# Second attention layer: row-tiled products in six runs per batch, the other products between them in a new order

## The chip, the cores and the metric

The kernel runs on one core of a Trainium2 chip. Its time is the device time of one execution in microseconds (us); the kernel before takes 1221.17 us, the median of three runs between 1220.6 and 1221.69. The core has five engines with a queue each: TensorE (PE; its weight loads are shown apart as PEld), VectorE (DVE), ScalarE (ACT), GpSimd (POOL) and SyncE (SP), which here only starts transfers. Each runs its own instructions in order and waits for the others by semaphores.

## The reference

The input is x, 16 batches of 256 tokens with 256 features, and a context of the same shape. Four layers are computed:

```
x = x + xattn0(layernorm(x), ctx, ctx)          # 16 heads of 16
x = x + moe(layernorm(x))                       # 8 experts, top 2
x = x + xattn1(ctx, layernorm(x))               # the layer of this change
x = x + ffn(layernorm(x))                       # relu, fp8 rounding
```

The third one, in full:

```
q = latents @ w_q.T                  # latents = layernorm(x), per batch 256 x 256
k, v = split(ctx @ w_kv.T)
attn = softmax(einsum('blhd,bshd->bhls', q, k) * 16 ** -0.5)
out = einsum('bhls,bshd->blhd', attn, v).reshape(B, L, 256)
out = out @ w_out.T + b_out
```

## The kernel before, in words

The four layers stand one after the other. The change is in `second_attention` alone (lines 1055 to 1731). It is a software pipeline over 16 batches, written out step by step: `body(b)` of each engine runs for b from -6 to 17, and inside it a loop over g from 0 to 7 goes over the eight pairs of heads. In each g there are two products whose contraction has 63 or 64 rows, so that two of them lie in the two halves of the TensorE array at once. These are the row-tiled products of the title:

- `row_max(m, gm)` (L1397), four matmuls: scores of a later batch, of which VectorE takes the maxima (`reduce`, L1673). In body b they belong to batch b+1 for g below 4 and to batch b+2 from g = 4.
- `score(b, g)` (L1408), four matmuls: scores of batch b with the maximum taken off through an extra row, of which ScalarE takes the exponential (`exp`, L1567).

The other products of a batch are spread over the same eight steps: `turn_norm` (L1438, transpose of the normalised rows of batch b+3), `project_q` (L1456, 12 matmuls, same batch), `turn_neg` (L1430, transpose of the negated maxima of batch b+1), four `pv` (L1421, probabilities times values for two pairs of heads each, 32 columns wide), `out_rows` (L1479, transposes of the result of batch b-1), `turn_att` (L1438 on att, batch b-2) and `project_out` (L1468, 12 matmuls, batch b-2).

Two rings of PSUM memory couple the engines. `big` has three banks, used in turn by row_max, score and out_rows, 17 uses per batch. A use may begin when the third last one has been read: by `reduce` on VectorE, by `exp` on ScalarE, or by the two VectorE instructions of `out_rows`. `spare` has two banks for the nine other products; each use waits for the reader of the one before the last: `pv_out` and `neg_out` on ScalarE, and a pair of ScalarE `hi_out` and VectorE `lo_out` for the turned and projected ones (`q_hi_out` L1585 and `q_lo_out` L1705, `lo_out` L1721), or `add_out` (L1727) on VectorE. A `pv` also waits for the exponentials of its two pairs of heads. The order of the uses is written in `spare_order` and `big_order`.

Round these: ScalarE scales gathered rows (`scale_rows`, L1591) and clears the stacked operands once at the start (`clear_k` L1550, `clear_q` L1554). GpSimd gathers the expert rows, combines them, takes the power for the layer norm (`power`, L1296), normalises (`apply`, L1303) and splits k. VectorE takes the statistics (`ln_stats`, L1679). SyncE copies q, k and the negated maxima into the stacked form that the row-tiled products read (`stack_q` and `stack_k` L1220, `stack_neg` L1240), loads rows and stores x3 (L1248). The first bodies, with b below 0, only fill the pipeline. The last two hold, between the last products, the first steps of the feed-forward layer (`ffn.turn` L935, `ffn.up` L947), whose operands lie in memory that the attention layer has given free.

## Time and profile before

| | us |
|---|---|
| median of 3 runs | 1221.17 |
| profiled execution, first to last instruction | 1218.4 |
| feed-forward layer, from 1098 to the end | 120.4 |
| middle of the second attention layer, one batch | 16.16 |

The profiled execution's own time is taken as the median of the runs: its span is 1218.4 us, and 2.8 us lie around it. Over the span PE is busy 1129.2 us (93%), DVE 908.6 (75%), ACT 743.3 (61%) and POOL 611.8 (50%). The second attention layer reaches from about 791 to 1098 us. A busy PE is not PE at its peak, since the ends of matmuls are modelled: what tells is the distance from the start of one group to the start of the next, and the idle time in brackets. In a line of the trace in order of time, "x4" means four instructions merged into one piece whose length is given.

### The profile page before, as it was taken

To read this page: it belongs to the slowest core of one execution; us is meant where nothing else is said; L and a number is where in the kernel's file an instruction comes from. 1 tells how busy PE (TensorE), PEld (TensorE's weight loads), DVE (VectorE), ACT (ScalarE), POOL (GpSimd) and SP (SyncE) were. 2 spreads that over 40 slices of the span, in tenths; PEclk is the share of its full clock that TensorE was granted. 3 is DMA by queue.
4 is the path that set the end of the run, shared out by engine and by line. 5 is a ranking of instruction groups with operands and counts; after the bars stand their busy time and mean duration, and the time that the engine had idled before them with its cause. 6 is when DMAs were issued, how large, how long until landed. Compare 5 with 4: busy or idle time off the path is not lost. (4 is left out here: it accounts for less than half of the span.)

```text
span 1218.4 us, 26789 instructions
## 1 busy us (share of the span) xinstructions
PE 1129.2 (93%) x9622; PEld 925.1 (76%) x9623; DVE 908.6 (75%) x1303; ACT 743.3 (61%) x983; POOL 611.8 (50%) x607
## 2 busy tenths in 40 slices
PE   3899999989899999999999999857999999999997
PEld 2566666679788999999999999745666666668886
DVE  7899999669488888878878777567888888743332
ACT  4687778856445555554555655365877887764442
POOL 3588777344686886722002000788877876002222
PEclk9999999989899999999999999956999999999999
DMA  6577766359936465523132111165656665402221
GB/s 216 202 254 249 268 237 227 132 201 355 325 127 195 142 190 167 174 100 113 43 112 69 34 52 43 55 229 185 216 196 217 208 229 183 155 28 70 69 69 35
DMA packets 121862, 194.19 MB, mean 159 GB/s; under 512 B 12208, under 2 KB 65456, under 8 KB 121648
## 3 DMA queue, kind: packets, MB, share of 16 engines
q1 hardware_dynamic: 105520, 148.57, 35.6%
q0 software_dynamic: 12656, 39.33, 10.3%
q10 hardware_dynamic: 3600, 5.12, 1.2%
q8 instruction: 55, 0.90, 0.3%
q14 instruction: 31, 0.25, 0.1%
HBM read 92.85 MB, written 51.12 MB: 118 GB/s over the span
## 5 line engine op out<-in xcount | busy, mean ns | idle before, releaser
L2389 PE MATMUL y_ps<-e_w,hiddenT_hi 128*128 x624 | 225.3, 403 | 1.9 <-DVE rows L2509 1.9
L2432 ACT ACTIVATE hidden<-hidden 128x1024 f32<-128x1024 f32 x78 | 82.8, 1062 | 190.6 <-DVE hidden L2470 168.1
L2372 PE MATMUL h_ps<-kvT_hi,tile_w_hi 128*128 128x256 f32 x624 | 179.2, 287 | 6.9 <-DVE kvT_lo L2492 6.9
L1673 DVE TENSOR_REDUCE neg_max<-big 128x4 fp32r<-128x1024 f32 x128 | 154.5, 1222 | 36.4 <-PE big L1397 33.8
L2372 PE MATMUL h_ps<-kvT_lo,tile_w_hi 128*128 128x256 f32 x624 | 178.5, 286 | 0.0
L2372 PE MATMUL h_ps<-kvT_hi,tile_w_lo 128*128 128x256 f32 x624 | 178.4, 286 | 0.0
L2390 PE MATMUL y_ps<-e_w,hiddenT_lo 128*128 x624 | 175.2, 281 | 0.0
L736 DVE TENSOR_REDUCE neg_max<-big 128x4 fp32r<-128x1024 f32 x128 | 155.1, 1217 | 23.3 <-PE big L485 22.0
L1567 ACT ACTIVATE probs<-big 128x1024 f32<-128x1024 f32 x128 | 130.7, 1023 | 46.2 <-PE big L1408 44.1
L644 ACT ACTIVATE probs<-big 128x1024 f32<-128x1024 f32 x128 | 130.6, 1022 | 44.3 <-PE big L496 44.2
L2498 DVE TENSOR_TENSOR hiddenT_lo<-hidden,hiddenT_hi 128x1024 fp32r<-128x1024 f32 x78 | 98.7, 1306 | 58.2 <-ACT hiddenT_hi L2443 53.7
L2389 PEld LDWEIGHTS y_ps<-e_w,hiddenT_hi 128*128 128x128 f32 x624 | 117.3, 188 | 29.5 <-issue 2.3
L2372 PEld LDWEIGHTS h_ps<-kvT_hi,tile_w_hi 128*128 128x128 f32 x624 | 121.7, 195 | 9.8 <-DVE kvT_lo L2492 5.8
L2372 PEld LDWEIGHTS h_ps<-kvT_hi,tile_w_lo 128*128 128x128 f32 x624 | 121.8, 195 | 0.0
L2372 PEld LDWEIGHTS h_ps<-kvT_lo,tile_w_hi 128*128 128x128 f32 x624 | 121.7, 195 | 0.0
L2462 DVE TENSOR_TENSOR tile_w_lo<-e_w,tile_w_hi 128x1024 fp32r<-128x1024 f32 x76 | 110.7, 1457 | 12.1 <-issue 6.7
L2390 PEld LDWEIGHTS y_ps<-e_w,hiddenT_lo 128*128 128x128 f32 x624 | 118.1, 189 | 0.0
L2470 DVE TENSOR_TENSOR hidden<-h_ps,e_b1T 128x1024 f32<-128x1024 f32 x78 | 95.2, 1221 | 24.9 <-PE h_ps L2372 21.1
L1825 POOL DMA_INDIRECT rows<-norm,token_of_slot x74 | 90.7, 1226 | 21.8 <-issue 21.8
L984 ACT ACTIVATE probs<-big,f_b1T 128x512 fp8e4<-128x512 f32 x64 | 44.0, 687 | 72.1 <-PE big L947 64.2
L2428 ACT ACTIVATE tile_w_hi<-e_w 128x1024 fp32r x76 | 75.8, 1045 | 6.5 <-issue 4.2
L1397 PE MATMUL big<-k_stack,q_stack 63*128 63x256 f32 x512 | 67.6, 348 | 12.1 <-DMA q_stack<-q_cut 6.9
(282 smaller groups left out, 2565.8 us busy)
## 6 DMA issues: line engine op xcount, KB each, us to landing
q_stack<-q_cut SPq DMA_DIRECT2D x96, 256.0 KB, 2.6
k_stack<-k_cut SPq DMA_DIRECT2D x72, 256.0 KB, 2.7
e_w<-in_L_ffn_w POOLq DMA_DIRECT2D x10, 1024.0 KB, 6.9
slots_out<-rows SPq DMA_DIRECT2D x39, 256.0 KB
slots_in<-rows POOLq DMA_DIRECT2D x37, 256.0 KB
slot_x<-slots_in SPq DMA_DIRECT2D x37, 256.0 KB
vals<-in_v_wide SPq DMA_DIRECT2D x16, 512.0 KB, 4.4
vals<-v_wide SPq DMA_DIRECT2D x16, 512.0 KB, 4.0
```

The lines of the kernel that those rows point to most:

```text
L644: nc.scalar.activation(probs[g][:], big[bank][:], ACT.Exp, scale=SCALE).then_inc(big_freed[bank], 1)
L736: nc.vector.tensor_reduce(neg_max[m % 2][:, :, :, g].rearrange("p q a -> p a q").bitcast(F32R), big[bank][:], AX.X, ALU.max, negate=True). ...
L1567: nc.scalar.activation(probs[g][:], big[bank][:], ACT.Exp, scale=SCALE).then_inc(big_freed[bank], 1)
L1673: nc.vector.tensor_reduce(neg_max[m % 2][:, :, :, g].rearrange("p q a -> p a q").bitcast(F32R), big[bank][:], AX.X, ALU.max, negate=True). ...
L1825: pool.indirect_dma_start(out=rows[:, q, :], out_offset=None, in_=dram["norm2"], in_offset=bass.IndirectOffsetOnAxis(ap=const["token"][:, ...
L2372: last = nc.tensor.matmul(h_ps[k][:, f % HF, :], w1[w][b.u][:, c, f * P:(f + 1) * P], xT[a][b.u][:, c, :], start=(n == 0), stop=(n == 3 * ...
L2389: nc.tensor.matmul(y_ps[q][:].rearrange("p s d -> p (s d)"), hT[0][o.u][:, f, rows], both, start=(f == 0), stop=False)
L2390: last = nc.tensor.matmul(y_ps[q][:, 0, :], hT[1][o.u][:, f, rows], both[:, 0:DIM], start=False, stop=(f == FC - 1))
L2432: nc.scalar.activation(half(hidden, k), half(hidden, k), ACT.Gelu).then_inc(gelu_done, 1)
L2462: nc.vector.tensor_tensor(w1[1][n.u][:, c, :], of_place(expert_w["w1"], c, places.of(n)), w1[0][n.u][:, c, :].bitcast(F32), ALU.subtract). ...
L2470: nc.vector.tensor_tensor(hidden[:, HF * k:HF * (k + 1), :], h_ps[k][:], bias.unsqueeze(2).to_broadcast([P, HF, SLOT_ROWS]), ALU.add).then ...
L2498: nc.vector.tensor_tensor(hT[1][b.u][:, half, :], hidden[:, half, :], hT[0][b.u][:, half, :].bitcast(F32), ALU.subtract).then_inc(hT_ready, 1)
```

## The change

Only the order of work changes; each instruction is still there, with the same operands and shapes.

- TensorE: where g is 1 or 5 (`AHEAD`), the row_max of that g is moved into the step before, behind that step's score, so that the 16 row-tiled products stand in six runs of three or two instead of eight of two. The others are put into the six gaps: pv 3 of the batch before and turn_att; turn_norm and pv 0; project_q; pv 1 and turn_neg; project_out; out_rows and pv 2. The feed-forward parts inside the loop keep their g.
- ScalarE and VectorE read the banks in the new order. `scale_rows` of batch b+5 runs at g = 6 and 7 of body b, where that of batch b+4 ran at g = 2. On VectorE q_lo_out goes from g = 7 to g = 4, out_rows from 4 to 7, add_out from 3 to 7. The reductions keep their places, one per g.
- SyncE: `stack_q` comes before `stack_neg` and `stack_k`, and the store of x3 comes last. GpSimd is left alone.

```diff
@@ -1059,7 +1059,7 @@
     PARTS = 3 * 16
     MAX_ROW = STACK - 1
     LN_STEPS = 2 * QT + 1
-    OUT_AT = 4
+    OUT_AT, AHEAD = 7, (1, 5)
     RAMP = EARLY_ROWS
     UP_BATCHES = 10, 11, 12, 13
     HALF = PAIRS // 2
@@ -1068,15 +1068,19 @@
 
         return divmod((b + 1) * PAIRS + g + HALF, PAIRS)
 
+    def maxima_with(b, g):
+
+        return [maxima(b, k) for k in (g, g + 1) if (k == g) != (k in AHEAD)]
+
     spare_order, big_order = [], []
     for b in range(FIRST, END):
         spare_order += [(name, t) for name, t in (
-            ("attT", b - 2), (("pv", 3), b - 1), ("oproj", b - 2), (("pv", 0), b), ("normT", b + 3), ("negT", b + 1),
-            (("pv", 1), b), ("qT", b + 3), (("pv", 2), b)) if has(t)]
+            (("pv", 3), b - 1), ("attT", b - 2), ("normT", b + 3), (("pv", 0), b), ("qT", b + 3), (("pv", 1), b),
+            ("negT", b + 1), ("oproj", b - 2), (("pv", 2), b)) if has(t)]
         for g in range(PAIRS):
-            m, gm = maxima(b, g)
-            big_order += [(name, t) for name, t in ((("max", gm), m), (("score", g), b), ("out" if g == OUT_AT else None, b - 1))
-                          if has(t) and name]
+            uses = [(("max", gm), m) for m, gm in maxima_with(b, g)]
+            uses.insert(0 if g in AHEAD else 1, (("score", g), b))
+            big_order += [(name, t) for name, t in (*uses, ("out" if g == OUT_AT else None, b - 1)) if has(t) and name]
     spares, bigs = Ring(spare_order, 2), Ring(big_order, 3)
 
     with ExitStack() as ctx:
@@ -1243,19 +1247,19 @@
             def body(b):
                 if has(b + 1):
                     load_v(b + 1)
-                if has(b - 2):
-                    read_spare(sp, ("oproj", b - 2))
-                    sp.dma_start(tiled(dram["x3"], b - 2), x_in[(b - 2) % 8][:]).then_inc(stored[b % 2], 16)
                 if has(b + 5) and b + 5 >= RAMP:
                     load_x(b + 5)
                 if has(b + 4):
                     load_k(b + 4)
+                if has(b + 3):
+                    stack_q(b + 3)
                 if has(b + 1):
                     stack_neg(b + 1)
                 if has(b + 3):
                     stack_k(b + 3)
-                if has(b + 3):
-                    stack_q(b + 3)
+                if has(b - 2):
+                    read_spare(sp, ("oproj", b - 2))
+                    sp.dma_start(tiled(dram["x3"], b - 2), x_in[(b - 2) % 8][:]).then_inc(stored[b % 2], 16)
                 if b + 1 in up_pieces:
                     c, cols = up_pieces[b + 1]
                     wait(sp, up_lo, UP_BATCHES.index(b + 1))
@@ -1481,49 +1485,51 @@
 
             def body(b):
                 for g in range(PAIRS):
-                    m, gm = maxima(b, g)
-                    if has(m):
-                        row_max(m, gm)
-                    if has(b):
+                    if g in AHEAD and has(b):
                         score(b, g)
+                    for m, gm in maxima_with(b, g):
+                        if has(m):
+                            row_max(m, gm)
+                        if g not in AHEAD and has(b) and (m, gm) == maxima(b, g):
+                            score(b, g)
                     if g == 0:
                         if b == BATCHES:
                             last_of_big(pe, turn_bank)
                             ffn.turn(pe, chunk0)
+                        if has(b - 1):
+                            pv(b - 1, 3)
                         if has(b - 2):
                             turn_att(b - 2)
                     elif g == 1:
-                        if has(b - 1):
-                            pv(b - 1, 3)
                         if b == BATCHES + 1:
                             ffn.up(pe, chunk0, EARLY_UP - 1)
                     elif g == 2:
-                        if has(b - 2):
-                            project_out(b - 2)
+                        if has(b + 3):
+                            turn_norm(b + 3)
+                        if has(b):
+                            pv(b, 0)
                         if b == BATCHES:
                             last_of_big(pe, up_bank)
                             pe.wait_ge(up_lo, len(UP_BATCHES))
                             for f in range(EARLY_UP // 2):
                                 ffn.up(pe, chunk0, f)
                     elif g == 3:
+                        if has(b + 3):
+                            project_q(b + 3)
+                    elif g == 4:
                         if has(b):
-                            pv(b, 0)
-                    elif g == OUT_AT:
-                        if has(b + 3):
-                            turn_norm(b + 3)
-                        if has(b - 1):
-                            out_rows(b - 1)
-                    elif g == 5:
+                            pv(b, 1)
                         if has(b + 1):
                             turn_neg(b + 1)
-                        if has(b):
-                            pv(b, 1)
+                    elif g == 5:
                         if b == BATCHES:
                             ffn.up(pe, chunk0, EARLY_UP - 2)
                     elif g == 6:
-                        if has(b + 3):
-                            project_q(b + 3)
-                    elif g == 7:
+                        if has(b - 2):
+                            project_out(b - 2)
+                    elif g == OUT_AT:
+                        if has(b - 1):
+                            out_rows(b - 1)
                         if has(b):
                             pv(b, 2)
 
@@ -1609,37 +1615,39 @@
                                 act.wait_ge(q_stacked[u], BATCHES // 2 * PARTS)
                             for c in range(KC):
                                 ffn.hi(act, chunk0, c)
+                        if has(b - 1):
+                            pv_out(b - 1, 3)
                         if has(b - 2):
                             hi_out(("attT", b - 2), "oproj", attT, att_hi)
                     elif g == 1:
-                        if has(b - 1):
-                            pv_out(b - 1, 3)
+                        if has(b + 3):
+                            hi_out(("normT", b + 3), "qT", normT, xT_hi)
                         if b == BATCHES + 1:
                             ffn.relu(act, chunk0, EARLY_UP - 1)
                     elif g == 2:
+                        if has(b):
+                            pv_out(b, 0)
                         if b == BATCHES:
                             for f in range(EARLY_UP // 2):
                                 ffn.relu(act, chunk0, f)
                     elif g == 3:
+                        if has(b + 3):
+                            q_hi_out(b + 3)
+                    elif g == 4:
                         if has(b):
-                            pv_out(b, 0)
-                    elif g == 4:
-                        if has(b + 3):
-                            hi_out(("normT", b + 3), "qT", normT, xT_hi)
+                            pv_out(b, 1)
+                        if has(b + 1):
+                            neg_out(b + 1)
                         if has(b + 3) and 0 < b + 3 < RAMP:
                             k_hi_out(b + 3)
                         if b + 3 == 0:
                             clear_k(1)
                     elif g == 5:
-                        if has(b + 1):
-                            neg_out(b + 1)
-                        if has(b):
-                            pv_out(b, 1)
                         if b == BATCHES:
                             ffn.relu(act, chunk0, EARLY_UP - 2)
                     elif g == 6:
-                        if has(b + 3):
-                            q_hi_out(b + 3)
+                        if has(b + 5) and b + 5 >= RAMP:
+                            scale_rows(b + 5, 0)
                         if b + 3 == 0:
 
...
@@ -1733,6 +1740,8 @@
                     if has(m):
                         reduce(m, gm)
                     if g == 0:
+                        if has(b + 3) and b + 3 < RAMP:
+                            apply(b + 3)
                         if b == BATCHES:
                             for c in range(KC):
                                 ffn.lo(dve, chunk0, c)
@@ -1741,20 +1750,17 @@
                             lo_out(("attT", b - 2), attT, att_hi)
                         if b == BATCHES + 1:
                             ffn.norm(dve, chunk1)
+                    elif g == 2:
+                        if has(b + 3):
+                            lo_out(("normT", b + 3), normT, xT_hi)
                     elif g == 3:
-                        if has(b - 2):
-                            add_out(b - 2)
-                        if has(b + 3) and b + 3 < RAMP:
-                            apply(b + 3)
                         if b + 3 == 0:
                             k_lo_out(0)
-                    elif g == OUT_AT:
+                    elif g == 4:
                         if has(b + 3):
-                            lo_out(("normT", b + 3), normT, xT_hi)
+                            q_lo_out(b + 3)
                         if has(b + 3) and 0 < b + 3 < RAMP:
                             k_lo_out(b + 3)
-                        if has(b - 1):
-                            out_rows(b - 1)
                     elif g == 5:
                         if b == BATCHES - 2:
                             ffn.convert_b2(dve)
@@ -1767,9 +1773,11 @@
                         if has(b + 4):
                             ln_stats(b + 4)
                             ln_var(b + 4)
-                    elif g == 7:
-                        if has(b + 3):
-                            q_lo_out(b + 3)
+                    elif g == OUT_AT:
+                        if has(b - 1):
+                            out_rows(b - 1)
+                        if has(b - 2):
+                            add_out(b - 2)
 
             for b in range(FIRST, END):
                 body(b)
```

TensorE in the middle of the layer, from the project_q of one body to the project_out of the next, before (each row one group of matmuls; L1421 is pv, L1438 on att is turn_att):

```order
L1397 MATMUL big_1<-k_stack_1,q_stack_1 128x256 x4
L1408 MATMUL big_1<-q_stack_1,k_stack_1 128x256 x4
L1421 MATMUL spare_1<-probs_1,vals_1 32x256 x8
L1397 MATMUL big_1<-k_stack_1,q_stack_1 128x256 x4
L1408 MATMUL big_1<-q_stack_1,k_stack_1 128x256 x4
L1438 MATMUL spare_1<-ident,att_1 128x128 x4
L1397 MATMUL big_1<-k_stack_1,q_stack_1 128x256 x4
L1408 MATMUL big_1<-q_stack_1,k_stack_1 128x256 x4
L1421 MATMUL spare_1<-probs_1,vals_1 32x256 x8
```

And now, from the row_max of g = 0 to that of g = 3 (lines are eight or four higher: L1401 is row_max, L1412 score, L1425 pv, L1442 turn_att or turn_norm):

```order
L1401 MATMUL big_1<-k_stack_1,q_stack_1 128x256 x4
L1412 MATMUL big_1<-q_stack_1,k_stack_1 128x256 x4
L1401 MATMUL big_1<-k_stack_1,q_stack_1 128x256 x4
L1425 MATMUL spare_1<-probs_1,vals_1 32x256 x8
L1442 MATMUL spare_1<-ident,att_1 128x128 x4
L1412 MATMUL big_1<-q_stack_1,k_stack_1 128x256 x4
L1401 MATMUL big_1<-k_stack_1,q_stack_1 128x256 x4
L1412 MATMUL big_1<-q_stack_1,k_stack_1 128x256 x4
L1442 MATMUL spare_1<-ident,normed_1 128x128 x4
L1425 MATMUL spare_1<-probs_1,vals_1 32x256 x8
L1401 MATMUL big_1<-k_stack_1,q_stack_1 128x256 x4
```

Two pairs with one product between them have become runs of three, with two products of unlike shape side by side behind each.

TensorE at the start of the layer, before, from the last matmul of project_q of batch 0 to the first of batch 1:

```order
L1456 MATMUL spare_1<-normT_hi,qoT_lo 128x256
L1397 MATMUL big_1<-k_stack_1,q_stack_1 128x256 x4
L1438 MATMUL spare_1<-ident,normed_1 128x128 x4
L1397 MATMUL big_1<-k_stack_1,q_stack_1 128x256 x8
L1456 MATMUL spare_1<-normT_hi,qoT_hi 128x256
```

And now, where turn_norm and the whole of project_q of batch 1 come before the first row_max of batch 0, and the first seven row_max follow in one row:

```order
L1460 MATMUL spare_1<-normT_hi,qoT_hi 128x256
L1460 MATMUL spare_1<-normT_lo,qoT_hi 128x256
L1460 MATMUL spare_1<-normT_hi,qoT_lo 128x256
L1401 MATMUL big_1<-k_stack_1,q_stack_1 128x256 x28
L1442 MATMUL spare_1<-ident,normed_1 128x128 x4
L1401 MATMUL big_1<-k_stack_1,q_stack_1 128x256 x4
```

The first row_max has moved behind all 12 matmuls of the second project_q.

TensorE at the end of the layer, before, from the last out_rows (batch 15) to the last turn_att, with a piece of the feed-forward's `up` between them:

```order
L1479 MATMUL big_1<-ident,outT_1 128x128 x8
L947 MATMUL big_1<-k_cut_1,w1T_hi 128x512 x2
L947 MATMUL big_1<-k_cut_1,w1T_lo 128x512
L947 MATMUL big_1<-k_cut_1,w1T_hi 128x512 x2
L947 MATMUL big_1<-k_cut_1,w1T_lo 128x512
L1438 MATMUL spare_1<-ident,att_1 128x128 x4
```

And now:

```order
L1483 MATMUL big_1<-ident,outT_1 128x128 x8
L1442 MATMUL spare_1<-ident,att_1 128x128 x4
L947 MATMUL big_1<-k_cut_1,w1T_hi 128x512 x2
L947 MATMUL big_1<-k_cut_1,w1T_lo 128x512
```

The last turn_att stands directly behind the out_rows whose result it reads.

## Rows read from the trace of the kernel before

**Rows 1.** Busy time by stretch: from, to, length, each engine busy (instructions), clock, DMA.
```profile
788.00:844.00 56.00, 33.82 (x198) 24.70 (x198) 35.41 (x54) 29.86 (x38) 45.06 (x42) 0.58 0.57 193
844.00:1061.00 217.00, 205.18 (x2275) 144.04 (x2273) 184.97 (x245) 170.51 (x259) 150.51 (x141) 1.00 0.60 203
```

**Rows 2.** TensorE in order of time, batches in mid layer: start, length, line, operation.
```profile
943.00 0.51 PE L1397 MATMUL big<-k_stack,q_stack 63*128 63x256 f32 x4
...
943.68 1.07 PE L1421 MATMUL spare<-probs,vals 128*32 128x256 f32 x16
944.68 0.51 PE L1397 MATMUL big<-k_stack,q_stack 63*128 63x256 f32 x4
945.02 0.41 PE L1408 MATMUL big<-q_stack,k_stack 64*128 64x256 f32 x4
945.52 0.63 PE L1438 MATMUL spare<-ident,att 128*128 128x128 f32 x4
946.08 0.50 PE L1397 MATMUL big<-k_stack,q_stack 63*128 63x256 f32 x4
946.56 0.50 PE L1408 MATMUL big<-q_stack,k_stack 64*128 64x256 f32 x4
946.99 1.07 PE L1421 MATMUL spare<-probs,vals 128*32 128x256 f32 x16
...
956.11 0.50 PE L1397 MATMUL big<-k_stack,q_stack 63*128 63x256 f32 x4
957.14 0.50 PE L1408 MATMUL big<-q_stack,k_stack 64*128 64x256 f32 x4 [0.53 <-issue]
...
959.16 0.51 PE L1397 MATMUL big<-k_stack,q_stack 63*128 63x256 f32 x4
```

**Rows 3.** TensorE in order of time, start of batch 1: two groups of one run.
```profile
848.18 0.46 PE L1408 MATMUL big<-q_stack,k_stack 64*128 64x256 f32 x4
848.45 0.43 PE L1397 MATMUL big<-k_stack,q_stack 63*128 63x256 f32 x4
```

**Rows 4.** VectorE in order of time, same stretch as rows 2.
```profile
943.55 1.23 DVE L1673 TENSOR_REDUCE neg_max<-big 128x4 fp32r<-128x1024 f32 x1 [0.30 <-PE big L1397]
944.70 0.68 DVE L1705 TENSOR_TENSOR q_cut<-spare,q_cut 128x512 fp32r<-128x512 f32 x1
```

**Rows 5.** ScalarE in order of time, start of the layer.
```profile
800.86 0.60 ACT L1585 ACTIVATE q_cut<-spare 128x512 fp32r<-128x512 f32 x1 [1.95 <-PE spare L1456]
...
810.14 0.57 ACT L1599 ACTIVATE normT_hi<-spare 128x512 fp32r<-128x512 f32 x1
```

**Rows 6.** TensorE in order of time, start of the layer.
```profile
807.27 0.79 PE L1397 MATMUL big<-k_stack,q_stack 63*128 63x256 f32 x4 [6.45 <-DMA q_stack<-q_cut]
...
814.36 1.65 PE L1397 MATMUL big<-k_stack,q_stack 63*128 63x256 f32 x12
...
820.42 1.11 PE L1438 MATMUL spare<-ident,normed 128*128 128x128 f32 x4
...
827.36 0.40 PE L1408 MATMUL big<-q_stack,k_stack 64*128 64x256 f32 x4
...
837.92 0.79 PE L1397 MATMUL big<-k_stack,q_stack 63*128 63x256 f32 x4 [2.60 <-issue]
```

**Rows 7.** VectorE in order of time, start of the layer.
```profile
814.22 0.74 DVE L1679 BATCH_NORM_STATS2 stat<-rows 128x6 f32<-128x256 f32 x2
```

**Rows 8.** SyncE queue, same stretch: one batch of query copies.
```profile
830.81 1.95 SPq L1220 DMA_DIRECT2D q_stack<-q_cut  x3
```

**Rows 9.** TensorE in order of time, end of the layer.
```profile
1083.46 0.36 PE L1468 MATMUL spare<-qoT_hi,attT_hi 128*128 128x256 f32 x1 [1.24 <-DVE attT_lo L1721]
...
1087.70 1.03 PE L1479 MATMUL big<-ident,outT 128*128 128x128 f32 x8
...
1089.95 0.62 PE L1438 MATMUL spare<-ident,att 128*128 128x128 f32 x4
```

More of the change, by code:

```diff
@@ L1649, in body @@
                     elif g == 7:
+                        if has(b + 5) and b + 5 >= RAMP:
+                            scale_rows(b + 5, 1)
                         if has(b):
                             pv_out(b, 2)
-                    if g == 2 and has(b + 4) and b + 4 >= RAMP:
-                        scale_rows(b + 4, 0)
-                        scale_rows(b + 4, 1)
-                        if b + 4 in (2, 3):
-                            clear_q(b + 4)
+                    if g == 2 and b + 4 in (2, 3):
+                        clear_q(b + 4)
             clear_k(0)
```

## Prediction

> **What bounds the kernel now.** Read the busy time by stretch first, since the share over the whole span mixes layers of different kinds. In the middle of the second attention layer TensorE is busy 205 of 217 us, VectorE 185 and ScalarE 171 [rows 1]; TensorE runs there at a granted clock of 1.00 (2.4 GHz). In the 56 us before, the layer's filling, it is busy only 34 us at a mean clock of 0.58, so mostly at 1.2 GHz. The two parts must be judged apart: in the middle TensorE sets the pace and VectorE is close behind it, in the filling nobody is busy and a chain from engine to engine sets it.
>
> Then read TensorE's starts in order of time [rows 2]. The same row_max comes at 943.00 and at 959.16: a batch takes 16.16 us. A pair of row-tiled products takes 0.68 (943.00 to 943.68), of which 0.34 is the first (944.68 to 945.02) and so 0.34 (with rounding 0.33) the second; a pv takes 1.00. Whatever is longer than that is waiting:
> - the score behind row_max at 956.11 comes after 1.03 instead of 0.34: 0.69 lost. Its bank is read by the reduction that stands behind out_rows and lo_out on VectorE.
> - turn_att comes 0.50 behind its score instead of 0.33: its spare bank is the one of project_q, which VectorE reads from 944.70 to 945.38 [rows 4]. 0.17 lost, and as much at turn_norm, behind add_out in the same way.
> - 946.08 to 946.56 is 0.48 instead of 0.34: 0.14 lost; and 946.56 to 946.99 is 0.43 instead of 0.33: the first group after standing costs 0.10 more, which happens twice.
>
> Together 0.69 + 2 x 0.17 + 0.14 + 2 x 0.10 = 1.37 us of waiting in 16.16.
>
> **The change in the middle of the layer.** It adds no work. Merging two runs into threes saves what a run costs at its ends. The rows show a step inside a run, from score to row_max, of 0.27 [rows 3]; that stretch is at the full clock. A run of three is then 0.34 + 0.27 + 0.33 = 0.94, and four of those with two pairs make 5.12 against 8 x 0.68 = 5.44: 0.32 saved. Nearest bounds: if the inner step costs 0.34 like the outer one, 0.04 is saved; if it is 0.23, 0.48. I take 0.32. For a gap between two other products of unlike shape (pv then turn_att, out_rows then pv) no row in the middle stands; I take pv's 1.00 in front of anything, and give each of the four such seams 0.1 either way.
>
> The stalls change places. I lay the products end to end at these starts and put each reader on its engine: a reader starts 0.05 after the group's end (0.50 after a first group's start), a reduction passes VectorE on after 1.15 and q_lo_out holds its bank 0.68 [rows 4].
> - The 0.69 goes: out_rows and add_out now run at g = 7, behind a reduction whose bank is wanted only three uses later, and out_rows is followed on TensorE by pv 2 with 1.00.
> - turn_neg now stands two uses behind project_q in the spare ring. From row_max at g = 4: the reduction starts after 0.55 and frees VectorE at 1.70, q_lo_out ends at 2.38, TensorE can go on at 2.43. It is there after 0.34 + 0.27 + 0.33 + 1.00 = 1.94. New wait 0.49.
> - pv 0 now comes at g = 2, one exponential earlier than before: it waits some 0.16 for exp of g = 1, which stands behind attT's hi_out.
> - the last score of the two runs score, row_max, score waits for a reduction: 0.06 and 0.24, each with 0.10 for the restart.
>
> That is 0.49 + 0.16 + 0.30 + 0.20 = 1.15. A batch: 16.16 - 1.37 - 0.32 + 1.15 = 15.62. With the turns a little longer behind each other I take 15.65, 0.51 less. Over ten batches (3 to 12) that is -5.1 us; with the seams and the inner step at their ends, -1.5 to -9. VectorE is busy 185 of 217 us, 13.8 per batch, which leaves it under 2 us of 15.65, so the reductions can't be driven much faster whatever TensorE saves.
>
> The Trainium skill, TensorEngine Tiling (Array Packing), Key Properties, says that changing the tiling mode drains TensorE. Counting 128-row, row-tiled and 32-column products as three modes, a batch changed mode 17 times and now 16 times, since the seams between pv and the transposes are changes too. By that rule nearly nothing is saved by merging, which is the second rival below. The trace agrees so far that a step inside a run is shorter; no row of it shows a seam.
>
> **The filling.** Here the order costs. Before, row_max of batch 0 starts at 807.27, once its q copies have landed [rows 6]. Now turn_norm and project_q of batch 1 come first. What they wait for does not come sooner: ScalarE reaches the hi_out of that batch at 810.14, 9.28 behind q_hi_out [rows 5], and in the new order the same number of clears and scalings lies between (clear_k(1) comes in where clear_q(2) goes out, of equal shape). So project_q of batch 1 ends as before at 814.36 [rows 6], and only then the first of eight row_max starts, 7.1 us later. Three had been issued by then. On VectorE the reductions follow at 1.15; the statistics of batch 2, at 814.22 before [rows 7], come behind three reductions, q_lo_out and k_lo_out: 814.36 + 0.60 + 3 x 1.15 + 2 x 0.60 = 819.6, so 5.4 later. turn_norm(2) followed them by 6.2 us (820.42) over GpSimd's power and normalising, now to about 825.4. Its project_q ends near 830.6, and SyncE puts three q copies (1.95 us, [rows 8]) ahead of the negated maxima that the first score needs. The first score thus comes at about 836 instead of 827.36, +9.
>
> Part of it comes back. Before, TensorE stood 2.60 us before 837.92, waiting for stacked operands [rows 6], which are in place by then in the new order; and the body of batch 0, mostly at the low clock before, falls later and half into the full clock if that returns at the same time, near 844. I lay the bodies at half and full speed and get +6 at batch 1, and +4.2 at batch 3. Bounds: 0 if the chains overlap as well as before, +8 if the clock comes back later by the 4 us or so that the busy stretch starts later and nothing returns.
>
> **The end.** The last turn_att stands directly behind out_rows: 1089.95 - 1087.70 = 2.25 us is what the chain over VectorE takes [rows 9], of which out_rows itself covers its length of 1.03 (before, `up` lay in the rest): 1.2 lost. The wait of 1.24 at 1083.46 goes, but laying the new order end to end as above (pv 1.00, transposes as in rows 2) `up` then waits 0.65 for the low part of its input, and ffn.turn 0.26 for its bank. In batch 15 row_max is gone and ScalarE sets the pace; pv 0 and pv 1 stand one exponential earlier, so each waits about 1 us. 1.2 - 1.24 + 0.65 + 0.26 + 2.0 = 2.9; I take +3.0 (0 to +5). The feed-forward behind it is TensorE's alone and moves with it.
>
> Edits costed at nothing: scale_rows a batch earlier (its rows were gathered a batch before; if not, ScalarE stands before an exp), the x3 store last in SyncE's queue (what is behind it is load_v and load_x for later batches, with over a batch of slack), and stack_k behind stack_q (k is needed a batch later).
>
> **Sum.** +4.2 - 5.1 + 3.0 = +2.1 on the span of 1218.4: 1220.5, and with the 2.8 us around it 1223.3, against a median of 1221.17. The measurement can tell about 0.2%, 2.4 us.
>
> **Rivals.**
> - The merged runs let TensorE go and the new waits vanish because readers are quicker than I lay them. Then a batch is near 16.16 - 1.37 - 0.32 + 0.3 = 14.8, -14 over ten, and with +7.2 at the ends 1214.5. For it: 1.37 us of waiting was there to be had. Against: the wait at turn_neg follows from three durations.
> - Slower: the seams between unlike products eat what merging saves. With the inner step at 0.34 (0.28 more) and 0.1 for the four seams together a batch takes 16.03, -1.3 over ten, +5.9 with the ends, 1227.1. It decides once a seam costs over 0.1. Against it: 0.27 in rows 3; for it: no seam in the middle shows.
> - The clock stays low longer: TensorE stands from 804 to 811 and before the first score, and the full level returns late. +8 instead of +4.2: 1227. It decides from a return later than about 850.
> - The filling costs nothing, since batch 0 catches up wholly behind VectorE: -5.1 + 3.0, 1219.1.
>
> **Chances.** My forecast 0.48 (1220 to 1226), new waits vanish 0.17, seams 0.12, late clock 0.13, free filling 0.10. Faster by over 0.2%: the second and half of the last with a little of the first, 0.26; within 0.2%: 0.38; slower by over 0.2%: 0.36. The range 1216 to 1228.5 leaves out the best of the second case and the worst of the third and fourth.
>
> **What would show it.** In the new trace: the row_max of g = 3 every 15.5 to 15.8 us in mid layer; idle time before turn_neg released by q_lo_out; no wait over 0.3 at the scores; the first row_max near 814 and the first score near 836; the full clock near 844; the last turn_att over 1 us behind out_rows' end; the feed-forward as long as before. I am wrong if the first score stays at 828, or if a batch takes under 15.2 or over 16.

## The result and the profile after

The changed kernel takes 1230.98 us (median of four runs, 1229.66 to 1235.58) against 1221.14 for the kernel before beside it: ratio 1.0095, 95% interval 1.0079 to 1.0110. It is slower, by 9.8 us, and lies outside the predicted range of 1216 to 1228.5. The profiled execution spans 1230.1 us, 11.7 more than before.

Where the time went is read from four marks: the first matmul of `project_q` of batch 0 (here "the layer's start"), the first `score` of batches 0, 1, 3 and 13, and the first `up` behind the last `project_out`. The layer's start lies between 796.5 and 801.4 us in the 17 profiles of this study, and just as far apart in the seven whose filling is the changed one up to there (799.0 on average, against 798.5 in the six with the old order), so everything below is counted from it.

| from the layer's start, us | before | after | difference | predicted |
|---|---|---|---|---|
| layer's start itself | 797.89 | 798.13 | +0.2 | 0 |
| to score of batch 0 | 29.47 | 40.07 | +10.6 | +9 |
| to score of batch 1 | 50.29 | 58.00 | +7.7 | +6 |
| to score of batch 3 (filling) | 82.42 | 90.64 | +8.2 | +4.2 |
| ten batches, 3 to 12 (middle) | 161.72 | 161.28 | -0.4 | -5.1 |
| from there to that `up` (end) | 51.66 | 55.11 | +3.5 | +3.0 |
| from `up` to the end of the program | 124.72 | 124.91 | +0.2 | 0 |

Busy time by stretch after (columns as in [rows 1]: from, to, length, PE, PEld, DVE, ACT, POOL, clock, DMA):

```profile
788.00:844.00 56.00, 27.99 (x144) 21.21 (x146) 30.81 (x50) 24.78 (x31) 37.84 (x36) 0.55 0.53 180
844.00:848.00 4.00, 4.00 (x30) 2.74 (x23) 1.92 (x2) 2.65 (x4) 3.56 (x4) 0.50 0.46 156
848.00:868.00 20.00, 16.87 (x198) 11.15 (x198) 15.56 (x19) 15.60 (x25) 15.71 (x15) 0.99 0.58 192
868.00:872.00 4.00, 3.93 (x28) 2.64 (x32) 3.51 (x9) 3.23 (x6) 3.23 (x5) 0.59 0.75 253
872.00:876.00 4.00, 4.00 (x53) 2.46 (x45) 2.70 (x3) 2.77 (x5) 3.71 (x4) 0.98 0.35 102
```

Up to 844 TensorE has 6 us less behind it than in [rows 1]. The full clock comes back at 848 instead of near 844, and at 868 to 872 the clock is mostly at 1.2 GHz once more, although TensorE was busy 16.87 of the 20 us before and never stood idle for more than 0.89 us in them. In those 4 us it has 28 matmuls, in the next four 53.

TensorE in the filling, pieces that stood still before (answers to [rows 6]):

```profile
798.13 0.58 PE L1460 MATMUL spare<-normT_hi,qoT_hi 128*128 128x256 f32 x1 [1.41 <-DVE normT_lo L1728]
...
814.59 1.65 PE L1401 MATMUL big<-k_stack,q_stack 63*128 63x256 f32 x12
...
826.13 1.12 PE L1442 MATMUL spare<-ident,normed 128*128 128x128 f32 x4 [2.84 <-POOL normed L1307]
...
838.20 0.80 PE L1412 MATMUL big<-q_stack,k_stack 64*128 64x256 f32 x4 [1.98 <-DMA q_stack<-neg_rows]
```

The first row_max stands at 814.59 (predicted 814.4), `turn_norm` of batch 2 at 826.13 (825.4), the first score at 838.20 (836), where it stood 1.98 us for the copies of the negated maxima.

TensorE in mid layer, one batch of 16.11 us from out_rows to out_rows (answers to [rows 2]; matmuls of the two projections left out):

```profile
951.07 1.09 PE L1483 MATMUL big<-ident,outT 128*128 128x128 f32 x8
952.09 1.07 PE L1425 MATMUL spare<-probs,vals 128*32 128x256 f32 x16
953.09 0.50 PE L1401 MATMUL big<-k_stack,q_stack 63*128 63x256 f32 x4
953.43 0.40 PE L1412 MATMUL big<-q_stack,k_stack 64*128 64x256 f32 x4
953.67 0.40 PE L1401 MATMUL big<-k_stack,q_stack 63*128 63x256 f32 x4
954.03 1.07 PE L1425 MATMUL spare<-probs,vals 128*32 128x256 f32 x16
...
956.63 0.66 PE L1442 MATMUL spare<-ident,normed 128*128 128x128 f32 x4
957.55 1.07 PE L1425 MATMUL spare<-probs,vals 128*32 128x256 f32 x16 [0.27 <-ACT probs L1573]
...
961.75 1.07 PE L1425 MATMUL spare<-probs,vals 128*32 128x256 f32 x16
963.33 0.29 PE L1434 MATMUL spare<-ident_r,neg_max 128*16 128x128 f32 x2 [0.51 <-DVE q_cut L1712]
963.54 0.50 PE L1412 MATMUL big<-q_stack,k_stack 64*128 64x256 f32 x4
963.88 0.40 PE L1401 MATMUL big<-k_stack,q_stack 63*128 63x256 f32 x4
964.46 0.50 PE L1412 MATMUL big<-q_stack,k_stack 64*128 64x256 f32 x4 [0.17 <-issue]
...
967.18 0.98 PE L1483 MATMUL big<-ident,outT 128*128 128x128 f32 x7
```

VectorE beside it (answers to [rows 4]):

```profile
961.45 1.23 DVE L1680 TENSOR_REDUCE neg_max<-big 128x4 fp32r<-128x1024 f32 x1 [1.12 <-issue]
962.59 0.68 DVE L1712 TENSOR_TENSOR q_cut<-spare,q_cut 128x512 fp32r<-128x512 f32 x1
```

And two products side by side that the new order has taken apart, in the trace of before, turn_norm and out_rows:

```profile
952.79 0.63 PE L1438 MATMUL spare<-ident,normed 128*128 128x128 f32 x4
953.25 1.04 PE L1479 MATMUL big<-ident,outT 128*128 128x128 f32 x8
954.22 0.50 PE L1397 MATMUL big<-k_stack,q_stack 63*128 63x256 f32 x4
```

The 1.03 of [rows 2] (score behind row_max, with 0.69 lost) is gone, and the step inside a run is 0.24 (953.43 to 953.67), shorter than the 0.27 I took. But turn_neg starts 1.58 behind pv instead of 1.00, pv 0 0.92 behind turn_norm instead of 0.59 (the distance from turn_att to its score), and the third product of a run 0.58 behind the second instead of 0.24.

The end (answers to [rows 9]):

```profile
1081.87 1.07 PE L1425 MATMUL spare<-probs,vals 128*32 128x256 f32 x16 [1.19 <-ACT probs L1573]
...
1084.54 1.07 PE L1425 MATMUL spare<-probs,vals 128*32 128x256 f32 x16 [0.93 <-issue]
...
1093.69 0.71 PE L947 MATMUL big<-k_cut,w1T_hi 128*128 128x512 f32 x2 [0.49 <-DVE k_cut L1035]
...
1099.29 1.03 PE L1483 MATMUL big<-ident,outT 128*128 128x128 f32 x8
1101.50 0.66 PE L1442 MATMUL spare<-ident,att 128*128 128x128 f32 x4 [1.18 <-DVE att L1722]
```

The first two are pv 0 and pv 1 of batch 15. turn_att stands idle 1.18 behind the last out_rows, the 1.2 of the prediction.

### The profile page after: what moved, and what is told of

Its sections match the earlier page's. It is cut to its first block and busy times, and to the rows that moved or that the text cites. A ratio compares the mean times of both kernels' runs of the same rounds, so it can differ in the third digit from the quotient of the medians.

```text
span 1230.1 us, 26789 instructions
## 1 busy us (share of the span) xinstructions
PE 1127.0 (92%) x9622; PEld 925.8 (75%) x9623; DVE 904.3 (74%) x1303; ACT 744.9 (61%) x983; POOL 608.7 (49%) x607
## 3 DMA queue, kind: packets, MB, share of 16 engines
q0 software_dynamic: 12656, 39.33, 10.9%
## 5 line engine op out<-in xcount | busy, mean ns | idle before, releaser
L736 DVE TENSOR_REDUCE neg_max<-big 128x4 fp32r<-128x1024 f32 x128 | 155.0, 1216 | 24.9 <-PE big L485 24.0
L2470 DVE TENSOR_TENSOR tile_w_lo<-e_w,tile_w_hi 128x1024 fp32r<-128x1024 f32 x76 | 106.4, 1400 | 14.8 <-issue 9.9
L1833 POOL DMA_INDIRECT rows<-norm,token_of_slot x74 | 86.3, 1166 | 21.8 <-issue 21.8
```

The costliest lines, as they stand in the source:

```text
L736: nc.vector.tensor_reduce(neg_max[m % 2][:, :, :, g].rearrange("p q a -> p a q").bitcast(F32R), big[bank][:], AX.X, ALU.max, negate=True). ...
L1833: pool.indirect_dma_start(out=rows[:, q, :], out_offset=None, in_=dram["norm2"], in_offset=bass.IndirectOffsetOnAxis(ap=const["token"][:, ...
L2470: nc.vector.tensor_tensor(w1[1][n.u][:, c, :], of_place(expert_w["w1"], c, places.of(n)), w1[0][n.u][:, c, :].bitcast(F32), ALU.subtract). ...
```

## The experiments

**The change by place.** Four kernels take the new order (on all engines and in both rings) in some bodies and the old one in the others; `NEW` has one of these four lines in each:

```diff
+    def NEW(b):
+        return b < 0                    # fill_new_only
+        return b >= 0                   # fill_old
+        return 0 <= b < BATCHES - 2     # middle_only
+        return b < BATCHES - 2          # end_old
```

fill_new_only: 

> New order only in the bodies below 0, in all four engines; bodies 0 to 17 in the old order. Theory A (the filling costs 8 us, by the later first row_max and by the clock that comes back 4 us later; the rest of the layer costs 3): +8 us against before, 1229, first score at 838. Theory B (the loss comes from the new order meeting itself, filling and middle together, and each part alone is nearly free): +2 or less, 1223.

fill_old: 

> Old order in the bodies below 0, new from body 0 on. Theory A: the 8 us of the filling go, what is left is -0.4 of the middle and +3.3 of the end: 1224. Theory B: 1228 or more stays.

middle_only: 

> New order only in bodies 0 to 13, old below and above. Theory A: 1220 to 1221.5, no change against before, since a batch takes 16.10 us where it took 16.17. Theory B: slower by over 2.

end_old: 

> New order up to body 13, old from body 14 on. Theory A: the 3.3 us of the end go, the 8 of the filling stay: 1227.5 to 1228.5. Theory B: 1231, as with the new order throughout.

| | us | ratio to before | to score 0 | to score 3 | batches 3 to 12 |
|---|---|---|---|---|---|
| fill_new_only | 1227.68 | 1.0068 (1.0051 to 1.0086) | 40.01 | 87.50 | 161.73 |
| fill_old | 1224.54 | 1.0044 (1.0027 to 1.0061) | 29.37 | 83.18 | 161.29 |
| middle_only | 1220.05 | 1.0002 (0.9989 to 1.0016) | 29.09 | 81.53 | 161.29 |
| end_old | 1228.44 | 1.0079 (1.0062 to 1.0096) | 39.33 | 87.98 | 161.38 |

The new order in the bodies below 0 alone puts score 3 back by 5.1 us (87.50 against 82.42) and makes the kernel slower by 0.68%. By time that is 7.7 us, near the 8 expected; what the profile doesn't show of it, 2.6, stays open. In the middle alone the new order changes nothing that can be measured, as expected. fill_old and middle_only differ only from body 14 on: 1224.54 against 1220.05, 4.5 us. In their profiles, counted from the layer's start, 3.2 lie behind score 13, in the end, and 1.65 ahead of score 3, where the code is the same: in fill_old the clock fell once more, 63.2 to 66.7 us after the layer's start, and in middle_only it didn't. end_old came as expected too.

**The place of the first row_max.** fill_place is the changed kernel with body -2 in the old order, in which row_max of batch 0 stands before the second `project_q`.

```diff
+    def NEW(b):
+        return b != -2
```

> New order throughout, but body -2 in the old one, so that the first two row_max of batch 0 stand again before project_q of batch 1. Theory (the place of the first row_max starts the loss in the filling): first score near 834 instead of 838, 3 to 4 us of the 8 regained, 1227. Rival (the clock, which returns late because TensorE has less to do in all the filling): less than 1.5 us regained, 1229.5 or more.

Measured 1228.57 (ratio 1.0061, 1.0041 to 1.0081). Counted from the layer's start (801.25 here), row_max came after 11.01 instead of 16.46, score 0 after 36.17 instead of 40.07 and score 3 after 84.44 instead of 90.64. Against 1230.98 that is 2.4 us back by time, and 4.1 by the ratios to the kernel before beside each (1.0061 against 1.0095), where the theory had 3 to 4 and the rival under 1.5. In the profile this one place carries 3.9 of the 10.6 us at the first score, and 6.2 of the 8.2 at batch 3; in those 6.2 is the clock, which came back 43.7 us after the layer's start instead of 50, and didn't fall again.

**The wait before turn_neg.** mid_qlo_early is middle_only with q_lo_out ahead of the reduction of g = 4 on VectorE, as the last thing of g = 3.

```diff
                         if b + 3 == 0:
                             k_lo_out(0)
-                    elif g == 4:
                         if has(b + 3):
                             q_lo_out(b + 3)
+                    elif g == 4:
```

> As middle_only (new order in bodies 0 to 13), but VectorE does q_lo_out before the reduction of g = 4 instead of behind it, in bodies 0 to 13. It takes away the wait of 0.58 us at turn_neg. Theory (VectorE has no room, a wait removed comes back at the next reduction): a batch 16.1 to 16.3, no gain against middle_only, the wait now at the score behind. Rival (TensorE's wait at turn_neg was a pure loss): a batch 15.55, 1214.

Measured 1222.36 (1.0019, 1.0005 to 1.0032) and 16.27 us a batch against 16.10. The wait before turn_neg is gone, and the two scores behind it wait instead:

```profile
955.63 0.51 PE L1449 MATMUL big<-q_stack,k_stack 64*128 64x256 f32 x4 [0.48 <-DVE neg_max L1834]
...
956.77 0.50 PE L1449 MATMUL big<-q_stack,k_stack 64*128 64x256 f32 x4 [0.39 <-DVE neg_max L1834]
```

VectorE now stands 1.29 us for ScalarE's half of q_cut before q_lo_out (970.02), with the reduction behind it. Here the wait that was moved within the ring didn't vanish; the next readers in the queue paid it.

**Cheaper reductions.** Each reduction reads only half the columns of its bank, in the order of before (half_reduce_old) and in the new one (half_reduce_new), so the maxima are those of half the keys.

```diff
-  ... big[bank][:], AX.X, ALU.max,
+  ... big[bank][:, :, :, 0:SEQ // 2], AX.X, ALU.max,
```

half_reduce_old: 

> The kernel before, its reductions in the second attention layer over half the columns (other values, VectorE freed of some 4.3 us per batch). It asks what TensorE's order costs with the readers out of the way: a batch 15.2 (16.16 less the waits of 0.69, 0.14 and 0.10).

half_reduce_new: 

> The changed kernel with the same halved reductions. Theory (merging saves about 0.3 per batch and its waits on VectorE ate it): a batch 14.9, 0.3 shorter than with the old order. Rival (the seams between unlike products eat the saving, waits or not): 15.2 or more, no shorter than with the old order.

Measured 1207.01 (0.9900, 0.9883 to 0.9917) with 15.23 us a batch, and 1214.46 (0.9957, 0.9941 to 0.9974) with 15.13. So waiting for VectorE costs both orders as much: half the reading gives back 0.93 and 0.97 us a batch. The old order came out as expected. The new one did not reach the 14.9 of the theory, nor was it as slow as the rival's 15.2: it is 0.10 better than the old one (0.06 over batches 3 to 12, 151.73 against 152.33). In the old order TensorE itself is what is left, busy 170.91 of 172 us from 876 on. In the new one (166.54) a wait for ScalarE at pv 0 remains, 0.44 where it was 0.33:

```profile
961.41 0.66 PE L1442 MATMUL spare<-ident,normed 128*128 128x128 f32 x4
962.44 1.07 PE L1425 MATMUL spare<-probs,vals 128*32 128x256 f32 x16 [0.37 <-ACT probs L1573]
```

**Runs of four.** mid_noahead is middle_only with `AHEAD` empty: the other products in the new places, the row-tiled ones in runs of 2, 4, 2, 2, 4 and 2.

> middle_only with AHEAD empty: the other products stand in the changed kernel's order, but no row_max is moved ahead, so that the row-tiled products stand in runs of 2, 4, 2, 2, 4 and 2 instead of 3, 3, 2, 3, 3 and 2. Theory: what a run may hold is set by the three banks of big and one reduction of 1.15 us for every second product; the fourth product of a run needs the bank whose reader has only just started, 0.7 us or more lost in each of the two runs of four: 17.0 to 17.8 us a batch instead of 16.10, 10 to 18 us more than middle_only's 1220.05, 1230 to 1238. Rival, that readers keep up with a run of four: 16.1 a batch, 1220.

Measured 1250.29 (1.0252, 1.0222 to 1.0281); a batch takes 17.93 or 19.4 us. The fourth product of a run waits for the reduction whose bank it takes:

```profile
963.32 0.40 PE L1438 MATMUL big<-k_stack,q_stack 63*128 63x256 f32 x4
964.55 0.50 PE L1449 MATMUL big<-q_stack,k_stack 64*128 64x256 f32 x4 [0.84 <-DVE neg_max L1834]
```

1.23 instead of 0.24, twice a batch, as the theory had it. The kernel came out slower still than the 1230 to 1238 expected, and the long batches show why. From, to, length, engines and clock, in a batch of 19.4 that begins at 941.2, near its start and in its last part:

```profile
938.00:950.00 12.00, 10.96 (x126) 7.71 (x125) 9.21 (x13) 8.75 (x15) 10.44 (x10) 1.00 0.58 186
...
956.00:957.00 1.00, 1.00 (x6) 0.81 (x4) 0.26 (x3) 0.38 (x1) 0.62 (x1) 0.50 1.02 385
957.00:958.00 1.00, 1.00 (x9) 0.93 (x8) 0.13 (x1) 0.00 (x0) 0.82 (x2) 0.50 0.58 223
```

From 954.8 to 958.2 the clock was at 1.2 GHz, and so it was for 3.4 us in four of the ten batches 3 to 12:

```profile
876.00:1048.00 172.00, 146.53 (x1563) 104.60 (x1556) 130.88 (x176) 121.35 (x185) 114.44 (x106) 0.96 0.56 183
```

TensorE is busy 147 of 172 us here, where it was 161 in the changed kernel and 164 before, both at 1.00. So without the two row_max moved ahead the new order loses 1.8 us a batch and more (17.93 or 19.4 against 16.10).

**The end.** end_up puts one piece of `up` back between the last out_rows and turn_att (and its relu on ScalarE behind the pv_out of g = 7).

```diff
-                    elif g == 5:
-                        if b == BATCHES:
-                            ffn.up(pe, chunk0, EARLY_UP - 2)
                     elif g == OUT_AT:
                         if has(b - 1):
                             out_rows(b - 1)
+                        if b == BATCHES:
+                            ffn.up(pe, chunk0, EARLY_UP - 2)
```

> The changed kernel, but the feed-forward's up and relu of EARLY_UP - 2 in body 16 move from g = 5 to g = 7, behind the last out_rows, so that they lie between out_rows(15) and turn_att(15) as they did before the change. Theory: the 1.18 us that turn_att(15) waits for VectorE is covered again, the changed kernel gets 1.0 to 1.2 us faster, so 1229.8 against 1230.98 (ratio to the kernel before near 1.0085). Rival: the exponentials of the last batch set the end, and up in the old place lay in time that was lost anyway; then nothing changes (within 0.3 us).

Measured 1229.10 (1.0080, 1.0053 to 1.0107). From the layer's start, the first `up` behind the last project_out comes after 305.87 instead of 307.03: 1.2 us, as expected. The time alone could not tell this.

**The clock.** warm_before and warm_after give TensorE work whose result nobody reads, in the filling: transposes, and each row_max of batches 0 and 1 three times.

```diff
+            def keep_busy(n):
+
+                for k in range(n):
+                    nc.tensor.transpose(big[2][:, k % 2, 0, 0:P], ident[:], ident[:])
...
             def row_max(m, g):
...
+                for again in range(2 if m < 2 else 0):
...
             def turn_norm(a):
+                if a < 2:
+                    keep_busy((20, 24)[a])
...
             def project_q(a):
+                if a < 2:
+                    keep_busy((4, 24)[a])
```

(In warm_before the last line has `(4, 0)[a]`.)

warm_before: 

> The kernel before with extra work for TensorE in the filling: transposes of the identity into an unused bank (20 and 24 of them ahead of turn_norm of batches 0 and 1, 4 ahead of project_q of batch 0), and each row_max of batches 0 and 1 computed three times instead of once. The result is the same. Before, the granted clock is 0.5 up to about 844 us with a short piece at 1.0. If the low clock costs time in the filling, the full level comes earlier, the bodies of batches 0 and 1 run at it, and the first out_rows comes 2 to 4 us sooner: 1217 to 1219 against 1221.1. If the chain over the other engines sets the filling and the clock costs nothing, the time is 1221 to 1224 (the extra work lies partly in the way).

warm_after: 

> The changed kernel with the same extra work for TensorE in the filling (24 transposes also ahead of project_q of batch 1, where the first row_max stood before). The changed kernel has the full clock from 848 us, and a second stretch at 0.5 at 869 to 872. Theory that the late clock is a large part of the 8.4 us which the first score of batch 3 came late: the full level comes by 842 and stays, and 3 to 5 us return: 1226 to 1228 against 1230.98. Rival, that only the order of the chain (first score 10.8 us late) makes the 8.4: under 1.5 us return, 1229.5 to 1232.

Measured 1219.44 (1.0003, 0.9981 to 1.0024) and 1231.27 (1.0101, 1.0074 to 1.0127). Neither is faster by time. In the profile of warm_before the full level is there from 26.9 us after the layer's start instead of 46.4, and score 3 comes 0.7 earlier (81.71), with score 0 2.8 later (32.25). The profile of warm_after shows a mean clock of 0.82 instead of 0.55 up to 844, the full level from there and no second fall:

```profile
788.00:844.00 56.00, 39.68 (x350) 34.38 (x349) 31.70 (x51) 25.82 (x33) 37.37 (x36) 0.82 0.55 184
844.00:848.00 4.00, 4.00 (x52) 3.10 (x48) 2.43 (x3) 3.03 (x5) 3.56 (x4) 1.00 0.30 99
...
868.00:872.00 4.00, 3.99 (x50) 2.66 (x47) 3.42 (x5) 3.16 (x7) 3.67 (x4) 1.00 0.61 189
```

Its score 3 came after 87.73 instead of 90.64. So both kernels ran again beside each other.

after_again: 

> The changed kernel again, more rounds, beside warm_after_again. Its second attention layer should start within 796 to 802 us in the profile, and from that start the first score of batch 3 comes 87.5 to 91 us later: near 90.7 where the granted clock falls to 0.5 once more at 868 to 872 us, near 88 where it doesn't. Time 1229 to 1231.5.

warm_after_again: 

> warm_after again, more rounds, beside the changed kernel on one chip. Theory: the fallen clock is worth 2.7 to 2.9 us of the layer (score of batch 3 at 87.7 instead of 90.7 from the layer's start); then the median lies 2 to 3.5 us under that of after_again. Rival: the extra work takes as much as the clock gives, or the clock falls only in some executions of the changed kernel: within 1 us of after_again.

Measured 1231.95 (1.0087, 1.0069 to 1.0105) and 1230.76 (1.0079, 1.0063 to 1.0095): within 1.2 us, with intervals that overlap. The time doesn't show that the clock can be bought back with extra work: in this second profile of the warmed kernel score 0 came 1.0 later than in after_again (41.04 against 39.99), and score 3 only 0.5 earlier (88.94 against 89.43), and the clock came back for good after 47.1 us, not 43.9, with as much extra work. What the clock itself takes is seen by comparing profiles of code that is the same up to body 13, from the layer's start:

| | clock back after | falls again | to score 0 | to score 3 |
|---|---|---|---|---|
| after | 50.1 | 70.6 to 74.0 | 40.07 | 90.64 |
| end_up | 50.2 | 70.6 to 74.0 | 40.07 | 90.69 |
| after_again | 50.0 | no | 39.99 | 89.43 |
| end_old | 47.2, with stretches at 1.0 before | no | 39.33 | 87.98 |

In the kernel before it came back after 46.4, in fill_new_only after 46.8. By these single profiles the second fall is worth 1.2 us (fill_old beside middle_only gives 1.4, since 0.3 of their 1.65 lay ahead of the fall), and the late return 1.4; both differ from one execution to the next.

**Two small gains together.** warm_mid is middle_only with the extra work, row_max repeated for batch 0 alone.

> middle_only (old order in the filling and at the end, new in bodies 0 to 13) with the extra work for TensorE in the filling, but row_max repeated for batch 0 alone. From the start of the layer, the first score of batch 13 came after 242.8 us in middle_only against 244.1 in the kernel before; with the full clock in bodies 0 and 1 another 0.7 us, the difference seen at batch 3 between warm_before and the kernel before. If both hold: ratio 0.998 to 0.999, 1218 to 1219 against 1220. If they don't add up: 1.000 within 0.001.

Measured 1222.61 (1.0020, 1.0009 to 1.0031): slower than before. Score 0 came after 32.21 instead of 29.09: 24 extra transposes (808.4 to 813.1) stand ahead of turn_norm of batch 1, which starts 14.2 us after the layer's start instead of 9.0. The gains don't add up. No kernel of this study beats the kernel before with the whole reductions.

## Why the prediction was wrong

**The sum.** On the span +2.1 was predicted and +11.7 measured, of the 9.6 between them 4.0 are the filling and 4.7 the middle. (Around the span lie 1.75 us, 1231.85 less 1230.1 for the profiled execution, not 2.8. By time the change costs 9.8: the profiled executions lie about 1 us under the median before and 1 us over it after.)

**The filling, +8.2 instead of +4.2: the term was mis-sized.** The chain was right step by step, to 0.2 at the first row_max, 0.7 at turn_norm of batch 2 (its own sum, 820.42 + 5.4, gives 825.8 and not 825.4) and 2.2 at the first score; fill_place shows that the order makes it. What failed is the way back. I laid +6 at batch 1 and a further 1.8 back by batch 3. Measured are +7.7 and +8.2; and in fill_new_only, whose clock came back as before, +5.1 at batch 1 and +5.1 at batch 3: behind batch 1 nothing returns. I also let the clock return near 844, as before; it returned at 848 and fell again. From the profiles the 8.2 part into 5.1 for the order in the bodies below 0 (fill_new_only, clock back as before), 0.5 for new bodies 0 to 2, which catch up a little less than old ones (end_old, 87.98 against 87.50), 1.4 for the late return and 1.2 for the second fall. So 1.4 more than I laid for the order, and 2.6 for the clock, each read from one profile. The late-clock rival has the size (+8 in all) right and its condition wrong: I let it decide from a return at 850, and 848 sufficed. Its size is in part luck, since it gave the clock 3.8, and of the 2.6 that are there 1.2 are a second fall that it doesn't have. Why the clock returned later the runs show only in part: TensorE had less to do in the same 56 us, 28 us against 34, and with extra work (40 and 41 us) it returned after 43.9 and 47.1 us; but end_old had it back after 47.2 with no more work than after_again. By time the clock's share isn't shown, since the extra work gave nothing back.

**The middle, -0.4 instead of -5.1: the terms that failed are the new waits, laid 0.30 too small, and the seams, put at nothing.** The waits of before went as predicted, and merging gave more than predicted: four runs of three take 0.94, 0.91, 0.92 and 0.91 without their waits, two pairs 0.67 and 0.68, together 5.03 against 5.44, so 0.41 instead of 0.32 saved. Against that:
- The new waits are 0.58 at turn_neg (0.49 laid), 0.33 at pv 0 (0.16), 0.34 at the last score of a run (0.30 for two) and 2 x 0.10 restarts: 1.45 against 1.15.
- Taking the transposes apart costs about 0.2. Before, turn_norm, with out_rows of the same shape behind it, took 0.46, and out_rows 0.97; now turn_norm with pv behind it takes 0.59, out_rows between a score and pv 1.02, and turn_att 0.59 instead of 0.56. I put the four seams at nothing, give or take 0.1 each. The 0.46 stood in the trace of before (952.79 to 953.25), beside the 0.56 of a turn with a row-tiled product behind it.

16.16 - 1.37 - 0.41 + 1.45 + 0.21 = 16.04, against 16.10 measured; 0.06 is left unnamed. The waits stand where I laid them, each longer by 0.1 to 0.2. In the trace, ScalarE comes to the exponential that pv 0 needs at 956.28, behind attT_hi, and VectorE takes a reduction (961.45) just ahead of the q_lo_out that turn_neg waits for, although the high half was ready at 961.60. mid_qlo_early shows that turning these two round only hands the wait on, and the halved reductions that waits for VectorE are worth some 0.95 us of a batch in either order, with TensorE's own work behind them in the old order and ScalarE at pv 0 in the new. The sentence of the prediction that VectorE has under 2 us of room in a batch was the right one, and I drew the wrong sum beside it.

The rule of the Trainium skill, TensorEngine Tiling (Array Packing), Key Properties, that a change of tiling mode drains TensorE, is borne out in part: a product inside a run takes 0.24, the first and the last one about 0.34, so entering or leaving the row-tiled form costs 0.1 each, and a turn with another shape behind it instead of more transposes 0.10 to 0.13 (0.56 and 0.59 against 0.46). By counting changes alone (17 before, 16 after) it came nearer to the measured middle than my sum did, but the 0.41 saved in the runs is there; the new waits and the transposes took it. The seams rival (16.03 a batch) came near the number by luck: the seams cost 0.2, where it had 0.1, and the inner step at 0.34, which is 0.28 of its 0.38, isn't there (0.24); waits stand in its place.

**The end, +3.5 instead of +3.0: right**, in its parts too: 1.18 at the last turn_att (end_up gives 1.2 back), `up` behind its input 0.49 (0.65 laid), ffn.turn 0.18 (0.26), pv 0 and pv 1 of batch 15 1.19 and 0.93 (about 1 laid for each). Not laid was 0.43 at pv 3 of batch 14. By time end_old is 2.5 us faster, 2.0 by the ratios (1.0079 against 1.0095), and fill_old against middle_only shows the 4.5 of which the profiles give 3.2 to the end; the intervals are 3 to 4 us wide each.

## What to carry to other kernels

Here a ring of banks joins three engines that are busy 96, 85 and 78% of the middle, and what the new order saved on the busiest one came back as waits in the ring. In such a case lay all the queues together, each reader behind what stands before it in its own queue, before a saved wait is counted. The filling of a pipeline is a case of its own; an order that is as good as the old one in the steady state can put its first product behind a chain that was hidden before. And compare profiles from a mark just ahead of the change: the layer's start wandered by 4.9 us, half of what was to be explained.

## What the runs showed of the hardware

- The granted clock isn't fixed by the program: in the same code it was back 47.2 to 50.2 us after the layer's start, and fell a second time in two of four profiles. Before that fall TensorE had been busy 16.87 of 20 us at the full level, without standing idle for more than 0.89 us; in after_again, where the clock stayed, it was busy 16.85 of the first 20. In mid_noahead it fell in every second or third batch of the layer, where no wait was longer than 0.85 us, and in the changed kernel between 876 and 1048 not once: with the waits of a run of four came a loss of clock on top, 19.4 us a batch instead of 17.93.
- A row-tiled product of four matmuls takes 0.24 us inside a run and 0.33 to 0.36 at its ends; four 128 x 128 transposes take 0.46 with more transposes behind them and 0.56 to 0.59 with another shape.
- Extra work raised the mean clock of every execution (0.977 to 0.986 over the program against 0.970 to 0.976 for the kernel before beside them) and didn't shorten the program by what the timing can tell.
